# Attention in a gated block: exponentials and turned scores bank by bank, and the split of the row maxima on GpSimd

## What is computed

```python
q, k, v = _proj(Wq, bq, x), _proj(Wk, bk, c), _proj(Wv, bv, c)   # per batch, then split in heads
q, k = _rope(q, 4), _rope(k, 4)
scores = jnp.einsum('bhqd,bhkd->bhqk', q, k) / jnp.sqrt(jnp.float32(kc))
p_attn = jax.nn.softmax(scores, axis=-1)
out = jnp.einsum('bhqk,bhkd->bhqd', p_attn, v)
out = out.transpose(0, 1, 3, 2).reshape(b, ch, t_t)
return _proj(Wo, bo, out)
```

## Time and profile before

| what | us |
|---|---|
| median of three runs | 1506.12 |
| lowest and highest | 1505.72, 1512.41 |
| the profiled execution | 1498.02 |
| its span, first to last instruction | 1496.0 |
| TensorE busy in the span | 1335.2 (89%) |
| VectorE busy | 925.2 (62%) |
| ScalarE busy | 753.8 (50%) |
| GpSimd busy | 683.2 (46%) |

### The profile page before, as it was taken

The page is one execution under the profiler, slowest core; times in us unless marked ns, Lnnn a source line. Parts: engine busy times, 40 slices in busy tenths (PEclk is TensorE's granted clock), DMA queues, the critical chain, the costliest instruction groups (busy, mean ns, idle before and its releaser), DMA issues. The chain is left out here.

```text
span 1496.0 us, 31398 instructions
## 1 busy us (share of the span) xinstructions
PE 1335.2 (89%) x10082; PEld 1003.1 (67%) x10083; DVE 925.2 (62%) x1685; ACT 753.8 (50%) x1205; POOL 683.2 (46%) x850
## 2 busy tenths in 40 slices
PE   4898999999998759999898999999957799999998
PEld 3444444444454348887787888888855688888887
DVE  7788888888898268665654333333324566666653
ACT  0477776777777643332343333333324666666652
POOL 7576767676764027544465433200044444554220
PEclk9999999999999969999999999999965899999999
DMA  3222222222221022111654333211161011111000
GB/s 99 81 72 79 71 79 71 78 77 76 79 74 48 3 90 99 47 53 68 193 178 159 95 95 91 69 51 53 46 216 29 7 36 43 43 28 43 15 15 29
DMA packets 88480, 107.61 MB, mean 72 GB/s; under 512 B 11280, under 2 KB 79248, under 8 KB 87760
## 3 DMA queue, kind: packets, MB, share of 16 engines
q1 hardware_dynamic: 78656, 74.57, 15.8%
q0 software_dynamic: 9744, 31.99, 6.7%
HBM read 54.10 MB, written 25.03 MB: 53 GB/s over the span
## 5 line engine op out<-in xcount | busy, mean ns | idle before, releaser
L406 DVE TENSOR_REDUCE row_max<-s_ps 128x4 f32<-128x1024 f32 x256 | 312.2, 1222 | 49.5 <-PE s_ps L553 44.5
L467 ACT ACTIVATE e_t<-st_ps 128x1024 f32<-128x1024 f32 x256 | 262.7, 1026 | 140.3 <-PE st_ps L553 140.3
L553 PE MATMUL st_ps<-q_st,k_st 32*128 32x256 f32 x1024 | 130.8, 331 | 45.6 <-DVE row_max L406 18.6
L569 PE MATMUL o_ps<-e_t,v_st 128*32 128x256 f32 x2048 | 166.2, 397 | 0.0
L553 PEld LDWEIGHTS st_ps<-q_st,k_st 32*128 32x128 f32 x1024 | 80.3, 187 | 103.9 <-issue 65.0
L1731 POOL DMA_INDIRECT gathered_tail<-sorted_results,result_at x64 | 70.3, 1098 | 154.1 <-POOLq L2222 135.8
L553 PE MATMUL s_ps<-k_st,q_st 32*128 32x256 f32 x1024 | 130.7, 342 | 5.9 <-DVE row_max L406 3.6
L1968 DVE TENSOR_TENSOR h_all_tail<-silu_tail,u_ps_tail 128x512 f32<-128x512 f32 x64 | 43.9, 685 | 122.0 <-ACT silu_tail L1839 66.7
L1589 PE MATMUL y_ps_moe<-w_all_moe,xt_hi_moe 128*128 x568 | 112.2, 281 | 4.7 <-DVE xt_lo_moe L1407 4.7
L1413 DVE TENSOR_TENSOR h_all_moe<-silu_moe,u_ps_moe 128x512 f32<-128x512 f32 x71 | 48.8, 687 | 108.9 <-PE u_ps_moe L1567 108.9
L1091 ACT COPY y_sb_moe<-y_ps_moe 128x256 f32<-128x256 f32 x71 | 26.5, 373 | 163.0 <-PE y_ps_moe L1589 163.0
(11 more groups left out here) (337 smaller groups left out, 3716.1 us busy)
## 6 DMA issues: line engine op xcount, KB each, us to landing
k_st<-k_part SPq DMA_DIRECT2D x96, 128.0 KB
q_st<-q_part SPq DMA_DIRECT2D x96, 128.0 KB
stage_moe<-in_experts POOLq DMA_DIRECT2D x21, 512.0 KB
rows_in_moe<-sorted_rows SPq DMA_DIRECT2D x71, 128.0 KB
sorted_results<-y_sb_moe SPq DMA_DIRECT2D x71, 128.0 KB
c_in<-in_ctx SPq DMA_DIRECT2D x32, 128.0 KB
x_sb<-in_x SPq DMA_DIRECT2D x32, 128.0 KB
xn_moe<-in_ctx SPq DMA_DIRECT2D x8, 512.0 KB
```

The source lines that it names most:

```text
L406: nc.vector.tensor_reduce(out, s_ps[p % 2][:], AX_X, ALU.max).then_inc(s["max_taken"], 1)
L467: nc.scalar.activation(e_t[t % 4][:], st_ps[:], ACT.Exp, scale=float(DH) ** -0.5)\
L553: last = nc.tensor.matmul(out, w, moving, start=True, stop=True)
L569: last = nc.tensor.matmul(o_ps[32 * j:32 * j + 32, u % 2, :], v_st[r][:, half_, u * UH + j, :], e_t[(2 * u + j // 2) % 4][:, j % 2, half_, :],
```

## The change

ScalarE's exponential of a step is now two, one for each PSUM bank, each with its own wait and its own mark on `exp_done`. TensorE writes the turned scores bank by bank: the first two of a step wait for the first bank to be read, the last two for the second, and `st_scored` is raised after each pair. The plain scores follow the same order, alternating with the turned ones, and are still marked once, at the end. All counts of `exp_done` and `st_scored` double.

`split_max` goes from VectorE to GpSimd, at the start of its round, and has three operations in place of two: the sign (into a new tile `m_whole`), the high part, the low part. On VectorE the row statistics go from step 2 to step 3.

```diff
+            def split_max(n, c):
+                pool.wait_ge(s["max_taken"], (n + 1) * STEPS)
+                wait_count(pool, s["m_turned"], n)
+                wait_alone(pool)
+                rows = row_max[c % 2][:].rearrange("p (j v) -> p j v", j=UH)
+                m = m_parts[:].rearrange("p (j l v) -> p j l v", j=UH, l=2)
+                nc.gpsimd.tensor_scalar(m_whole[:], rows, -1.0, None, ALU.mult).then_inc(s["m_turned_sign"], 1)
+                pool.wait_ge(s["m_turned_sign"], n + 1)
+                wait_alone(pool)
+                nc.gpsimd.tensor_copy(m[:, :, 0, :].bitcast(F32R), m_whole[:]).then_inc(s["m_high"], 1)
+                pool.wait_ge(s["m_high"], n + 1)
+                nc.gpsimd.tensor_tensor(m[:, :, 1, :].bitcast(F32R), m_whole[:], m[:, :, 0, :], ALU.subtract)\
+                    .then_inc(s["m_split"], 1)
...
             def body(n, c, i):
+                if there(n, c, 0):
+                    split_max(n, c)
                 if there(n, c, 3):
                     pool.wait_ge(c_loaded[(c + 3) % RING], 16 * uses(c, i, 3))
...
                 for p in range(STEPS):
-                    if p == 0 and there(n, c, 0):
-                        split_max(n, c)
                     if there(n, c, 1):
                         take_max(n, c, p)
                     if p == 0 and there(n, c, -2):
                         normalize_out(n - 2, 1)
-                    if p == 2 and there(n, c, 3):
+                    if p == 3 and there(n, c, 3):
                         stats_of(n, c, i, 3)
...
-                        act.wait_ge(s["st_scored"], g + 1)
                         if t % 2 == 0:
                             wait_count(act, s["pv_done"], 2 * UNITS * (n + k) + 2 * (t // 2) - 2)
-                        nc.scalar.activation(e_t[t % 4][:], st_ps[:], ACT.Exp, scale=float(DH) ** -0.5)\
-                            .then_inc(s["exp_done"], 1)
+                        for b in range(2):
+                            act.wait_ge(s["st_scored"], 2 * g + b + 1)
+                            nc.scalar.activation(e_t[t % 4][:, b, :, :], st_ps[:, b, :, :], ACT.Exp, scale=float(DH) ** -0.5)\
+                                .then_inc(s["exp_done"], 1)
...
-                for half_ in range(2):
-                    for at in range(2):
+                for at in range(2):
+                    for half_ in range(2):
...
-                    wait_count(pe, s["exp_done"], STEPS * (n + k) + t)
+                    wait_count(pe, s["exp_done"], 2 * (STEPS * (n + k) + t) - 1)
                     wait_alone(pe)
...
-                for at in range(0, 4, 2):
-                    for of, done in ((turned, "st_scored"), (plain, "scored")):
-                        for out, w, moving in of[at:at + 2]:
-                            last = nc.tensor.matmul(out, w, moving, start=True, stop=True)
-                        if of and at == 2:
-                            last.then_inc(s[done], 1)
+                for at in range(4):
+                    if turned:
+                        if at == 2:
+                            wait_count(pe, s["exp_done"], 2 * (STEPS * (n + k) + t))
+                        out, w, moving = turned[at]
+                        last = nc.tensor.matmul(out, w, moving, start=True, stop=True)
+                        if at % 2 == 1:
+                            last.then_inc(s["st_scored"], 1)
+                    if plain:
+                        out, w, moving = plain[at]
+                        last = nc.tensor.matmul(out, w, moving, start=True, stop=True)
+                        if at == 3:
+                            last.then_inc(s["scored"], 1)
```

More of the change, by code:

```diff
@@ L125, in attention @@
         row_max = [sb(f"row_max{r}", [P, 2 * HP]) for r in range(2)]
+        m_whole = sb("m_whole", [P, UH, 2 * UNITS])
         m_parts = sb("m_parts", [P, 4 * HP])
@@ L151, in attention @@
                  "q_projected q_roped q_summed q_whole q_high q_split k_projected k_roped k_summed k_whole k_high k_split "
-                 "v_projected v_stored scored max_taken m_high m_split m_turned m_taken "
+                 "v_projected v_stored scored max_taken m_turned_sign m_high m_split m_turned m_taken "
                  "st_scored exp_done pv_done o_taken o_turned rcp_ready o_normed a_turned a_taken "
@@ L226, in body @@
                     r = (c + 2) % RING
-                    wait_count(sp, s["st_scored"], STEPS * (n - 1))
+                    wait_count(sp, s["st_scored"], 2 * STEPS * (n - 1))
                     if isinstance(n, int) and n == -2:
@@ L254, in body @@
                     r = (c + 3) % RING
-                    wait_count(sp, s["st_scored"], STEPS * n)
+                    wait_count(sp, s["st_scored"], 2 * STEPS * n)
                     sp.wait_ge(s["k_high"], n + 4)
@@ L388, in rope_parts @@
                                         rope[:].rearrange("p a t -> p (a t)"), ALU.mult).then_inc(s[a + "_roped"], 1)
-            def split_max(n, c):
-                dve.wait_ge(s["max_taken"], (n + 1) * STEPS)
-                wait_count(dve, s["m_turned"], n)
-                rows = row_max[c % 2][:].rearrange("p (j v) -> p j v", j=UH)
-                m = m_parts[:].rearrange("p (j l v) -> p j l v", j=UH, l=2)
-                nc.vector.tensor_scalar(m[:, :, 0, :].bitcast(F32R), rows, -1.0, None, ALU.mult).then_inc(s["m_high"], 1)
-                dve.wait_ge(s["m_high"], n + 1)
-                nc.vector.scalar_tensor_tensor(out=m[:, :, 1, :].bitcast(F32R), in0=rows, scalar=-1.0,
-                                               in1=m[:, :, 0, :], op0=ALU.mult, op1=ALU.subtract).then_inc(s["m_split"], 1)
             def take_max(n, c, p):
@@ L562, in use_values @@
                     if half_ == 0:
-                        pe.wait_ge(s["exp_done"], STEPS * (n + k) + 2 * u + 2)
+                        pe.wait_ge(s["exp_done"], 2 * (STEPS * (n + k) + 2 * u + 2))
                         if u == 0:
```

## The result

| | before | after |
|---|---|---|
| median | 1505.92 us (1505.26 to 1512.41, 4 runs) | 1487.25 us (1485.1 to 1489.07, 4 runs) |
| the profiled execution | 1498.02 | 1487.29 |
| its span | 1496.0 | 1485.6 |

The changed kernel takes 0.9875 times as long, 95% interval 0.9846 to 0.9905: 1.2% less, 18.7 us between the medians, 10.7 us between the profiled executions. The forecast was 1496; 1487.25 lies just under its range.

What follows compares the result with a forecast made beforehand. No engine is full; waits between engines set attention's 14.78 us period. A 14.40 us GpSimd loop gives -10.8, the start +1.5, the last steps -1, together -10: 1496 us against the 1506.1 median, range 1488 to 1518.

Steps and rivals of the forecast that it cites:

- GpSimd loop: Attention: the split on GpSimd closes a loop from q_bare through addition, split, TensorE and VectorE back, 14.40 us a tile.
- The scores' loop: Attention: score groups and bank exponentials waiting on each other give a period of 14.17 to 14.69 us.
- x: TensorE's one other piece after each step's score group and value matmuls, 0.30 to 0.91 us each, 5.29 a tile.
- The inner wait: Second half of a score group waits for the second bank, 1.69 us after the previous step began, or 1.87 with longer release.
- rival 1: Little is won: inner wait releases in 0.25 or bank exponentials don't overlap; period 14.7 to 15.1, 1504 to 1515 us; 28%.
- rival 3: Strips block each other in the new matmul order: 0.12 us more per step, 1508 to 1511 us; 12%.
- Step 3's wait for `q_roped` is gone: TensorE in attention: with the statistics a step later on VectorE, behind the rotation, step 3 no longer waits.
- The sum: Period 14.40, -0.38 times 28.4 periods is -10.8 us; start about +1.5, last 13 steps -1; together -10.
- The step that failed: Whole kernel: the 8 us between profiled execution and median was carried over, giving 1488 against one and 1496 against the other.
- 2 (GpSimd takes over): A longer split on GpSimd sets attention's period: at 2.8 us T is 16.2, time 1546; at 1.7, 1515; 15%.
- the row at 0.83: Last stage: a GpSimd operation on 128x4 took 0.83 us; at that for each operation the split is 2.8.

Runs made afterwards that it cites:

- e6: Changed kernel with GpSimd's split of the next tile's maxima moved ahead of the addition to x; 1473.56 us, ratio 0.9828 to the kernel before.
- e7: Changed kernel with one more 128x256 addition, result unused, on GpSimd ahead of the addition to x; 1501.9 us, ratio 1.0039 to the kernel before.
- e3: Changed kernel with split_max back on VectorE and the statistics back in step 2, so the banks alone; 1480.46 us, ratio 0.9847 to the kernel before.
- e5: Changed kernel with the split of the maxima back on VectorE, statistics left in step 3; 1473.31 us, ratio 0.9847 to the kernel before.
- e10: Kernel before with only the changed kernel's matmul order in a score group, one wait, mark and exponential; 1501.49 us, ratio 1.0023.
- e4: Kernel before with only split_max moved to the start of GpSimd's round, in three operations; 1501.36 us, ratio 0.9991.
- e1: Kernel before, unchanged, run and traced once more; 1504.29 us, ratio 0.9996.
- e2: Changed kernel, unchanged, run once more; 1490.47 us, ratio 0.9886 to the kernel before.
- e8: Kernel before with four unused plain score matmuls per step added on TensorE in the last thirteen attention steps; 1496.2 us, ratio 0.9981.
- e9: e6 with the wait for the second bank as an instruction of its own ahead of the matmul; 1481.11 us, ratio 0.9882 to the kernel before.

## Why the prediction was right and wrong

**The loops.** Right, and near in the terms of the GpSimd loop. The GpSimd loop was forecast at 14.40 and is 14.42 in the mean; round one period the split took 1.00 as forecast (0.32, 0.21 and 0.25 against 0.31, 0.21 and 0.24), the stretch from `q_bare` to the end of the addition 10.15 against 10.06, the hand-over to TensorE 0.11 against 0.25, and the rest 3.12 against 3.09 (0.30, 1.01, 0.91, 0.09, 0.69, 0.09). That this loop binds was argued before and is shown by e6 and e7: an order that takes the addition to x out of it shortens the period, an operation put into it lengthens it. GpSimd's idle time before `q_bare` is 2.07 (2.1 forecast, 3.54 before). TensorE's wait before the maxima came out at 0.72 instead of 0.5; it takes the place of the wait for the second bank in step 2 (that group takes 0.44, 272.06 to 272.50, and 0.73 in e3).

**The scores' loop.** The forecast let TensorE run at 14.17 by it, with the statistics in step 3. The kernels that have them there and no GpSimd loop in the way show 14.02 (e5, e6). The difference is small because two errors of opposite sign lie in it. The first is x, the piece between a step's values and the next scores: it was taken as the recorded length (0.66 for the output turned, 0.44 for the attention turned, 0.70 for the output projection), where the distance to the next start is 0.59 (251.83 to 252.42 in e3), 0.37 (260.53 to 260.90 above) and 0.63 (262.17 to 262.80 in e3). The Trainium skill says on "Perfetto Trace Analysis", Tensor Engine Instruction, that the end of a matmul in a profile is estimated and not observed; the front of this document says the same of the recorded end, and the working used it all the same. Since the output is turned twice, these are four pieces, each 0.07 too long; the values are too long by 0.04 or more (267.48 to 268.15 in the changed kernel), and the maxima, 0.32 to the next scores (271.74 to 272.06), were 0.02 too short.

The second error is in the waits, which the working put at 0.80 in all (0.24 in step 4, 0.18 in step 0, 0.02 in step 1, 0.36 in step 2): pieces that are shorter leave more to wait for. In a tile of e6 the group of step 4 is held up by 0.28 (254.34 to 255.06, against 0.44), that of step 0 by 0.18 (261.60 to 262.22), and there is 0.07 in step 7 (259.85 to 260.36) and another 0.07 before the k projection, which the working doesn't have. Its 0.18 in step 0 stands there without a reason; in e6 it comes from the pair of exponentials of step 7, which starts 0.79 behind its scores (259.85 to 260.64) after two other operations of ScalarE. With the GpSimd loop longer than either value, none of this reached the forecast.

**The inner wait.** The mechanism (second bank 0.06 behind the pair of exponentials) is in the trace as forecast, 0.06. A group that is held up ends 0.43 after its second bank starts (254.09 to 254.52), so the wait counts in full, as the working had it. The price of a longer release was right as a slope and rested on too high a base: forecast 14.17 to 14.69 for 0.19, 2.7 per unit; measured 14.02 to 14.24 for 0.08, 2.7 too. So rival 1 (little is won) did not come: the release was short and the pair overlapped (1.08, as forecast). A release of 0.25 there was not seen.

**Strips and order.** The forecast took 0, rival 3 took 0.12 per step. The groups are as forecast (0.44), but e10 shows that the order isn't free: 0.14 a tile, since the exponential's scores are complete later. By the rule behind rival 3, which the Trainium skill states on "TensorE: Matmul & The Clock Gate", The mechanism (matmuls strictly in order of issue), the group would have been longer in the new order; the trace disagrees with it, with 0.45 in e10 and 0.44 before. In the changed kernel the price of e10 should be smaller, since the exponential of the first bank needs only the first half; that wasn't measured apart.

**The statistics.** "Step 3's wait for `q_roped` is gone": true. With the split on VectorE this is worth nothing (e3, e5), since step 4 then waits longer for its second bank; the working has this wait, at 0.24, and it measured 0.28. What neither the working nor the expectation of e4 says is that the move shortens the GpSimd loop: with the statistics in step 2 the stretch from the maxima to `q_bare` is 3.46 and not 3.12 (e4). The changed kernel with the statistics left in step 2 would then have a period of about 14.42 + 0.34 = 14.76, no better than the kernel before. This is an estimate from e4 and the changed kernel; no run has tried it.

**The sum.** The terms of the forecast make -10.3, taken as -10. In the profiled executions attention gave 11.9 and the rest took back 1.5. The q additions from the fifth to the last divide the 11.9. Before and after:

```profile
L304 POOL TENSOR_TENSOR q_bare<-q_roped x28: 723/726/728, 74.8 to 471.0; 128x256 f32<-128x256 f32 x28
```

```profile
L305 POOL TENSOR_TENSOR q_bare<-q_roped x28: 723/727/731, 72.3 to 461.6; 128x256 f32<-128x256 f32 x28
```

| | forecast | measured |
|---|---|---|
| start, to the fifth addition | +1.5 | -2.5 |
| 27 periods (28.4 in the forecast) | -10.8 | -6.9 |
| from the last addition to the last exponential | -1 | -2.5 |
| behind attention | 0 | +1.5 |

The loop's term was too large because 14.78 is the period of one tile; the mean of 20 was 14.73, and over all 27 it is 396.2 / 27 = 14.67. The start is not a gain that can be put down to the change: it differs by 3.5 us between two executions of the kernel before (fifth addition at 74.8 and, in e1, at 71.3). TensorE's clock rises at different times there: the eight value matmuls of a step take 1.08 us, as in e1's last steps at a clock of 0.52, until the step at 59.89 in the first trace and until the one at 57.90 in the changed kernel, and in e1 they take 0.64 from 52.41 on. Against the profiled execution the same sum, 1488, met 1487.3. With the loop 3.9 too large and the start 4.0 too small, that is luck in part.

**The step that failed** is the last one: "the median of the runs is 1506.1, 8 above; the same sum gives 1488 against the one and 1496 against the other". It carried the distance between the profiled execution and the median over to the changed kernel. After, the median and the profiled execution are 1487.25 and 1487.29. The 8 us come and go with the execution: e1, 13.9 us longer than the first trace, has 12.2 of them behind attention, in stages that the change doesn't touch, with places at a lower granted clock. On another chip the kernel before had a median of 1497.86. Beside e1 ran 23 executions of the kernel before: the eight with a mean clock of 0.960 or more took 1499.3 to 1504.6, the ten with 0.955 or less 1504.1 to 1509.1. The six executions of e2 all have 0.960 to 0.966 and a median of 1490.5, 12.2 under the median of those eight (1502.7) and 15.1 under that of all 23. So some 11 to 12 us are the change (10.7 in the first pair of profiled executions), and the rest of the 15.1 goes along with the clock. For the 18.7 of the first medians the same is likely, but the clocks of those executions of the kernel before, the profiled one apart, are not on record. Why the kernel before loses clock more often stays open. That the thin last steps are the cause was tried (e8): the spread fell, the median by 1.7 us with an interval that holds 0. The exponentials by banks don't keep the clock up by themselves either: three of the six executions of e3 have 0.954 or less. By the later runs the changed kernel takes 1.1% less (e2), with this share of the clock in it.

**The rivals.** 2 (GpSimd takes over) has the mechanism right and the size too large, by the row at 0.83; it is what keeps the changed kernel from the 14.02 of e5 and e6. e7 shows the slower side of it: 0.61 more on GpSimd and the gain is gone. 3 is refuted at its size (e10).

## What to carry to other kernels

When an operation moves to another engine, write down the loop that it closes there, through every engine and with all that stands ahead in their programs. Beside whole exponentials the move costs nothing (e4), beside exponentials by banks 0.4 us a tile (14.42 against the 14.02 of e5), since it depends on which loop is longest beside it. Where the loop can't be avoided, put the operation ahead of work that nobody waits for (e6). Sum a chain from distances between starts, not from lengths, and make a forecast against several executions of the kernel before, since one median of three can stand 8 us off.

## What the runs showed of the hardware

- A wait in an instruction of its own costs TensorE more than one on the matmul itself: 0.14 against 0.06 behind ScalarE (e9, e3), and 0.24 for the outer wait before the change.
- Two exponentials of 128x512 back to back take 1.08 to 1.10, one alone 0.598: the second starts 0.1 before the recorded end of the first.
- Matmuls on different strips seem to start out of the program's order. In a group that isn't held up, the four turned matmuls start at 252.42, 252.43, 252.64 and 252.66 (e3), each with a plain one. In one that is held up, the first bank's two start 0.21 apart (253.79 and 254.00) and the second bank's only at 254.09. Two matmuls on the same strip don't start together there, so the early pair of a free group should hold one of each bank, although the program has both of the first bank's ahead. Step 7's groups say the same. In e3 its turned matmuls start at 250.72, 250.83, 250.94 and 251.05, and the one at 250.83 comes 0.05 behind a pair of exponentials (249.68 + 1.10), for which only the second bank's wait. In e9, with the longer release, they start at 252.84, 252.96 and 253.06: the second is later, and the third still 0.22 behind the first. The records don't name the bank, so this is inferred from the start times.
- The clock of the same kernel differs from one execution to the next in stages that have the same work: 1.00 and 0.97 from 750 to 950 us in the two traces of the kernel before, and 1.00 and 0.52 in its last attention steps (e1).
- In e7 TensorE's clock falls for short times between 120 and 440 us, which no other trace shows, and the period is 15.33 over all of it against 15.00 where there is no fall. TensorE is about as busy in attention there (90.8 of 100 us from 200 to 300) as in the kernel before (90.8), whose clock stays at 1.00; why it fell was not followed up.
